# Layer 1's gelu as a tanh on ScalarE and a product on VectorE, with new ticks

## The chip, the cores and the metric

One of the eight cores of a Trainium2 chip runs the whole program. The metric is the device time of one execution in microseconds. The engines are called PE (TensorE, matrix products), ACT (ScalarE, functions of one operand), DVE (VectorE), POOL (GpSimd) and SP (the queue that issues the transfers).

## The reference, cut to what matters

Four layers are applied to x, 32 sequences (called items here) of 256 tokens by 256 channels: layer 0, two conditioned norms with a silu and a matrix product each; layer 1, a transformer block with 16 heads, an attention bias and a mask; layer 2, a stencil; layer 3, a causal transformer block. The change touches the feed-forward part of layer 1, whose width is 1024:

```
def _gelu2(x):
    return x * jax.nn.sigmoid(1.702 * x)
...
x = x + (ctx @ Wo + bo)
h = _ln(x) * g2 + beta2
ff = _gelu2(h @ W1 + b1) @ W2 + b2
return x + ff
```

Layer 3 has the same form with the exact gelu. It is identical in both kernels.

## The kernel before

All weights lie in SBUF, and the 32 items go through one long software pipeline. The order of the work is written out in ticks. Each piece of an item's work ("w1", "f1", ...) has a tick relative to the item's start; items start 64 ticks apart (PERIOD), and layer 3 of an item starts 160 ticks (S3) after its layer 1. The table P holds the ticks of the steady state, OWN replaces them for the first and last items, SPLIT has those that differ for attention in layer 3. Every engine goes through all the ticks in order and issues what falls on each; within one tick the attention comes first. So ticks set only the order of the instructions on each engine's queue. What waits for what across engines is set by semaphores. Attention has eight units per item and layer, four ticks apart, so one unit runs every four ticks.

The part around the change, for item b, with its ticks in P:

- Layer 1's rows of normed input are turned by PE into the bank bM (t2, 55). ACT writes their high half as fp16 into MB (t2_out, 52), and DVE the rest (t2_lo, 55). MB is the same tile as TN, which layer 3 of an earlier item uses in the same way (t4_out, lines 1370 to 1373, waits until layer 1's w1 has read MB).
- PE multiplies with W1 in four steps g, two ticks apart (w1, 57 to 63; line 1447), all into the one bank bM. After each step ACT copies it with its bias into AA[g], 128x512 fp32 as two halves (w1_out, 57 to 63; lines 1343 to 1347, the copy itself is line 1275). The next step on PE waits for that copy.
- ACT applies the gelu to each AA[g] in place (w1_gelu, 64; lines 1348 to 1352), four instructions of 128x512, with the per-tensor scale of the split weights. The function is Gelu_apprx_sigmoid, which needs a table of functions that the exp of the attention (line 1249) isn't in.
- PE multiplies AA[g] with W2 in four steps, one tick apart (w2, 68 to 71; line 1525 through `narrow`), each waiting for its gelu.
- DVE adds the result to x (f1, 74; line 1116), and the stencil of layer 2 follows from there (s_r, s_rp, ...; POOL has s_pm, s_b, s_ha).

Others that the prediction speaks of: DVE's `all_center` (line 969, pieces n1_center and n2_center), POOL's addition of the mask to the attention bias (mask_add, line 579, tick -23, 128x1024, one for each of the eight units), POOL's addition of a bias row to x (m1_b, line 617, tick 56), SP's load of the attention bias (ld_bt, -12), and WARM, which lists extra matmuls on a constant tile that PE executes at named places.

The four lines of the gelu:

```
for b in at(t, "w1_gelu"):
    for g in range(4):
        S.wait_ge(a_w1, 8 * b + 2 * g + 2)
        S.op.activation(AA[g][:, :], AA[g][:, :], ACT.Gelu_apprx_sigmoid,
                        scale=scale_of("w1", 0)).then_inc(a_h1, 1)
```

Of the kernel before, what the change touches and what calls it, by code (L numbers as in the profile page):

```python
# [49 lines left out]
def begin(layer, b):  # L50
# [6 lines left out]
    "score0": -1, "score1": -1, "bias0": 0, "bias1": 0, "exp0": 1, "exp1": 2, "flip0": 8, "flip1": 8, "ev0": 7,  # L57
    "ev1": 9, "pv": 14, "cx": 13, "ct": 17, "pvn": 17, "ld_bt": -12, "mask_add": -23, "stack": -8, "ld_x": -78,
    "ld_xn": -37, "ld_ab": -36, "ld_mask": -117, "mask": -34, "n1_stats": -75, "n1_ones": -69, "n1_sum": -69,
# [6 lines left out]
    "f1": 74, "s_pm": 63, "s_b": 67, "s_r": 75, "s_rp": 82, "s_re": 96, "s_ha": 81, "s_w": 97, "s_ab": 97,  # L66
    "s_row": 98, "s_mm": 103, "s_f": 103, "ld_w1": -24, "ld_sten": -46, "ld_w3": -277, "coefs": -21,
# [6 lines left out]
    "out": 74, "st_out": 71,  # L74
# [32 lines left out]
        "y3": 60, "m4_rstd": 249, "m4_b": 298, "ld_x": -76, "ld_xn": -71, "ld_ab": -70, "ld_mask": -17,  # L107
        "ld_bt_1": -13, "stack_1": -12, "s_row": 96, "stack_3": -39, "st_out": 840,
    },
# [7 lines left out]
        "t2_lo": 70, "f1": 89, "s_r": 94, "s_rp": 94, "s_re": 94, "s_ab": 99, "s_f": 104, "m3": -54, "t3_lo": -37,  # L117
# [7 lines left out]
        "m4_b": 656, "ld_x": -88, "ld_xn": -61, "ld_ab": -39, "ld_mask": -139, "ld_bt_1": -22, "stack_1": -17,  # L125
        "stack_3": 217, "st_out": 980,
    },
# [10 lines left out]
        "s_rp": 86, "s_re": 97, "s_w": 99, "s_ab": 102, "s_f": 109, "t3_lo": -44, "bias1_3": 0, "v3_out": 15,  # L138
# [1701 lines left out]
```

## Time and profile before

| what | us |
|---|---|
| median of 3 runs | 2604.91 (2603.47 to 2608.86) |
| the profiled execution | 2604.97 |
| its span, first to last instruction | 2603.7 |
| PE busy | 2470.5 |
| ACT busy | 2115.3 |
| DVE busy | 2043.6 |
| POOL busy | 1536.1 |

The durations below come from the profiled execution. The busy time of an engine is the time in which at least one of its instructions runs; matmuls are pipelined, and their ends are modelled. A timeline row has the start, the time up to the end of the last instruction of the row, and, in brackets, the idle time of the engine before it with what ended it.

### The profile page before, as it was taken

What the parts mean: (1) busy time and instruction counts of PE and PEld (TensorE: products, weight loads), DVE (VectorE), ACT (ScalarE), POOL (GpSimd) and SP (SyncE); (2) the same over time, 40 slices, a digit from 0 to 9 for tenths busy, and PEclk for the clock granted to TensorE, in tenths of its full rate; (3) what the DMA queues carried; (4) which work ended last, traced back from release to release, by engine and by line L of the source; (5) the groups of instructions that cost most, each with busy time, mean ns of one, the idle gap of its engine ahead of it and who ended that gap; (6) DMA issues with size and microseconds to landing.
All of it is one profiled execution on the core that took longest, in us unless ns stands there. A gap on an engine that the chain in (4) does not pass through costs nothing.

```text
span 2603.7 us, 57961 instructions
## 1 busy us (share of the span) xinstructions
PE 2470.5 (95%) x19148; PEld 2005.6 (77%) x19148; DVE 2043.6 (78%) x7387; ACT 2115.3 (81%) x4694; POOL 1536.1 (59%) x1487
## 2 busy tenths in 40 slices
PE   6878999999999999999999999999999999999987
PEld 5666778778877877887887788778878877877776
DVE  6787878788888778888787888878888888878653
ACT  2466888888898888889888888988888888888875
POOL 2566666556666656666665656666556576655421
PEclk6899999999999999999999999999999999999999
DMA  5433443333344333334443333444433344433211
GB/s 205 120 119 105 121 127 113 111 106 106 107 122 126 112 110 108 107 105 122 126 115 108 108 107 106 122 127 115 114 110 100 105 121 125 123 105 96 75 29 33
DMA packets 178537, 287.67 MB, mean 110 GB/s; under 512 B 46080, under 2 KB 99328, under 8 KB 177984
## 3 DMA queue, kind: packets, MB, share of 16 engines
q1 hardware_dynamic: 178240, 283.97, 38.5%
q8 instruction: 155, 2.54, 0.4%
q14 instruction: 142, 1.16, 0.2%
HBM read 174.64 MB, written 8.45 MB: 70 GB/s over the span
## 4 chain that ended last, share of the span: by engine, by line
PE 69%; DVE 15%; SPq 4%; ACT 4%; issue 3%; POOL 2%; DMA 2%; DVEq 0%; POOLq 0%; ACTq 0%
PE bank L1525 17%; PE bank L1447 12%; PE bank L1548 10%; PE bank L1538 6%; PE bank L1563 6%; PE bank L1507 6%; DVE PB L1010 4%; PE bank L1514 3%; SPq L496 3%; PE bank L1459 3%; PE bank L1701 2%; DVE bank L969 2%; PE bank L1436 2%; SPq L492 1%; DMA Ks<-KU 1%
## 5 line engine op out<-in xcount | busy, mean ns | idle before, releaser
L1249 ACT ACTIVATE PB<-PB,mx 128x256 f32<-128x256 f32 (+1 forms) x2048 | 831.4, 473 | 35.7 <-DVE mx L1010 34.7
L579 POOL TENSOR_TENSOR BT<-BT,MN 128x1024 f32<-128x1024 f32 x256 | 556.9, 2180 | 122.5 <-DMA BT<-in_bias 121.0
L1548 PE MATMUL bank<-ident,PB 128*128 128x128 f32 x3584 | 486.4, 274 | 11.5 <-ACT PT L1254 5.5
L1010 DVE CUSTOM_DVE_ANT_0 PB<-bank,BT 128x256 f32<-128x256 f32 x1024 | 372.0, 418 | 137.8 <-PE bank L1538 132.8
L1548 PEld LDWEIGHTS bank<-ident,PB 128*128 128x128 f32 x3584 | 421.6, 141 | 63.4 <-ACT PB L1249 10.6
L1447 PE MATMUL bank<-TN,WS_w 128*128 128x256 f16 x3072 | 378.8, 273 | 38.7 <-ACT BB L1275 19.6
L1538 PE MATMUL bank<-Ks,Qs 96*128 96x512 f32 (+1 forms) x1024 | 364.6, 430 | 25.5 <-DMA Ks<-KU 12.0
L1017 DVE COPY PT<-bank 128x512 f32<-128x512 f32 (+1 forms) x512 | 315.9, 617 | 87.5 <-PE bank L1548 85.8
L1447 PEld LDWEIGHTS bank<-TN,WS_w 128*128 128x128 f16 x3072 | 282.5, 98 | 120.1 <-ACT BB L1275 35.4
L1254 ACT ACTIVATE PT<-bank 128x512 f32<-128x512 f32 (+1 forms) x512 | 272.3, 532 | 94.9 <-PE bank L1548 90.6
L1010 DVE CUSTOM_DVE_ANT_0 PB<-bank,caus 128x128 f32<-128x128 f32 (+1 forms) x1024 | 306.6, 350 | 42.3 <-PE bank L1538 42.2
L1563 PE MATMUL bank<-PT,VW 128*32 128x256 f32 (+1 forms) x4096 | 248.2, 360 | 4.4 <-DVE CX L1027 2.4
L1525 PE MATMUL bank<-Wf,BB 128*128 128x256 f32 x1024 | 236.8, 379 | 0.8 <-ACT BB L1264 0.6
L1525 PE MATMUL bank<-Wf,AA 128*128 128x256 f32 x1024 | 236.0, 383 | 0.5 <-ACT AA L1351 0.4
L1538 PEld LDWEIGHTS bank<-Ks,Qs 96*128 96x128 f32 x1024 | 168.1, 192 | 67.7 <-DVE mx L1010 22.3
L1525 PEld LDWEIGHTS bank<-Wf,AA 128*128 128x128 f32 x1024 | 192.2, 191 | 29.5 <-issue 0.9
L1525 PEld LDWEIGHTS bank<-Wf,BB 128*128 128x128 f32 x1024 | 189.6, 190 | 25.1 <-issue 1.7
L1563 PEld LDWEIGHTS bank<-PT,VW 128*32 128x32 f32 x4096 | 107.5, 109 | 98.7 <-issue 49.0
L554 POOL TENSOR_SCALAR smm<-smm 128x2 f32<-128x2 f32 x32 | 7.2, 226 | 280.0 <-DVE smm L991 280.0
L1010 DVE DVE_READ_ACCUMULATOR2_ANT mx<- 128x1 f32 x2048 | 169.0, 83 | 0.0
L1275 ACT ACTIVATE BB<-bank,cols 128x256 f32<-128x256 f32 x256 | 107.4, 470 | 44.3 <-PE bank L1447 44.3
L1260 ACT ACTIVATE ET<-bank 128x256 f32<-128x256 f32 x256 | 97.2, 380 | 46.8 <-PE bank L1563 42.7
(285 smaller groups left out, 4735.9 us busy)
## 6 DMA issues: line engine op xcount, KB each, us to landing
BT<-in_bias SPq DMA_DIRECT2D x256, 512.0 KB, 4.3
Qs<-QH SPq DMA_DIRECT2D x512, 64.0 KB, 2.4
Ks<-KH SPq DMA_DIRECT2D x1024, 32.0 KB, 2.0
Qs<-QU SPq DMA_DIRECT2D x256, 64.0 KB, 2.4
Ks<-KU SPq DMA_DIRECT2D x512, 32.0 KB, 2.0
XT<-in_xT SPq DMA_DIRECT2D x32, 256.0 KB, 2.8
X<-in_x SPq DMA_DIRECT2D x32, 256.0 KB, 2.9
AB<-ada_rows SPq DMA_DIRECT2D x32, 256.0 KB, 3.7
```

The costliest lines, as they stand in the source:

```text
L579: G.op.tensor_tensor(v2(BT[k % 4]), v2(BT[k % 4]), MN[:, :].unsqueeze(1).broadcast_to([128, 2, 512]), ALU.add).then_inc(g_bt, 1)
L1010: V.op.tensor_tensor_reduce(PB[(2 * D + q) % 6][:, h * 256:h * 256 + w], bS[q][:, h * w:h * w + w], plus, -1.0, 3.0e38, ALU.add, ALU.min, ...
L1017: V.op.tensor_copy(flipped(u.D, 1)[:, 0:w], bP[1][:, 0:w]).then_inc(v_ev, 1)
L1249: S.op.activation(o, o, ACT.Exp, scale=-1.0, bias=mx[u.layer][:, c:c + 1]).then_inc(a_exp, 1)
L1254: S.op.activation(flipped(u.D, 0)[:, 0:w], bP[0][:, 0:w], ACT.Copy).then_inc(a_ev, 1)
L1275: S.op.activation(half(out, m), half(ps, m), ACT.Identity, scale=scale(m), bias=bias(m)).then_inc(sem, 1)
L1447: last = T.op.matmul(half(ps, m), w, v[:, k * 256:k * 256 + 256], start=(k == 0 and i == 0), stop=(k == 1 and i == 2))
L1507: last = T.op.matmul(half(ps, m), x[:, k * 256 + m * 128:k * 256 + m * 128 + 128], Wf[:, a + k * 256:a + k * 256 + 256], start=(k == 0), s ...
L1525: last = T.op.matmul(half(ps, q), x[:, f * 256 + q * 128:f * 256 + q * 128 + 128], Wf[:, c:c + 256], start=(g == 0 and f == 0 and q == 0), ...
L1538: T.op.matmul(bS[q][:, 0:2 * w].rearrange("p (h k) -> p h k", h=2), Qs[i][0:96, et * 256 + q * 128:et * 256 + q * 128 + 128], k2[:, :, 0:w ...
L1548: last = T.op.transpose(bP[h][:, c * 128:c * 128 + 128], PB[(2 * u.D + q) % 6][:, h * 256 + k * 128:h * 256 + k * 128 + 128], ident[:, :])
L1563: last = T.op.matmul(half(bV, J % 2)[32 * s:32 * s + 32, q:256], VW[x][:, v:v + 32], flipped(u.D - 1 + et, h)[:, k * 256:k * 256 + 256 - q ...
```

## The change

Layer 1's gelu is x * sigmoid(1.702 x) = 0.5 x (1 + tanh(0.851 x)). ACT now computes the tanh of a half (128x256) of AA[g] into a half of MB, eight times per item, and DVE computes (tanh + 1) * AA[g] in place (new piece h1, tick 67). The factor 0.5 goes into f1, which becomes a three-operand instruction with a pointer scalar. Two scales are made for this once, in the set-up. w2 waits for DVE's product (v_h1) and no more for ACT. MB is in use until the last product, so ACT's tanh waits for all four steps of w1, each tanh waits for the product of the half before last, and layer 3's t4_out waits for the products.

```
@@ def split_gains
+                if n == "w1":
+                    V.op.tensor_scalar(scale_of(n, 4), scale_of(n, 0), 0.851, None, ALU.mult).then_inc(v_ws, 1)
+                    V.op.tensor_scalar(scale_of(n, 5), scale_of(n, 0), 0.5, None, ALU.mult).then_inc(v_ws, 1)
@@ def middle (DVE)
+                for b in at(t, "h1"):
+                    for g in range(4):
+                        for i in range(2):
+                            V.wait_ge(a_h1, 8 * b + 2 * g + i + 1)
+                            V.op.scalar_tensor_tensor(out=half(AA[g], i), in0=half(MB, i), scalar=1.0, in1=half(AA[g], i),
+                                                      op0=ALU.add, op1=ALU.mult).then_inc(v_h1, 1)
                 for b in at(t, "f1"):
...
-                    V.op.tensor_tensor(x[:, :], bM[:, :], x[:, :], ALU.add).then_inc(v_f1, 1)
+                    V.op.scalar_tensor_tensor(out=x[:, :], in0=bM[:, :], scalar=scale_of("w1", 5), in1=x[:, :], op0=ALU.mult,
+                                              op1=ALU.add).then_inc(v_f1, 1)
@@ def scalar (ACT)
                 for b in at(t, "w1_gelu"):
+                    S.wait_ge(p_w1, 4 * b + 4)
                     for g in range(4):
                         S.wait_ge(a_w1, 8 * b + 2 * g + 2)
-                        S.op.activation(AA[g][:, :], AA[g][:, :], ACT.Gelu_apprx_sigmoid,
-                                        scale=scale_of("w1", 0)).then_inc(a_h1, 1)
+                        for i in range(2):
+                            S.wait_ge(v_h1, 8 * b + 2 * g + i - 1)
+                            S.op.activation(half(MB, i), half(AA[g], i), ACT.Tanh, scale=scale_of("w1", 4)).then_inc(a_h1, 1)
...
                 for b in at(t, "t4_out"):
-                    S.wait_ge(p_w1, 4 * min(b + 3, NB))
+                    S.wait_ge(v_h1, 8 * min(b + 3, NB))
@@ def tensor (PE)
                 for b, g in steps(t, "w2", 4, 1):
-                    T.wait_ge(a_h1, 4 * b + g + 1)
+                    T.wait_ge(v_h1, 8 * b + 2 * g + 2)
@@ WARM
-    "start": 24, "c1": 12, "n1_ones_0": 2, "v1": 9, "win_1": 5, "w1_0": 3, "n2_ones_2": 1, "n1_ones_3": 4,
-    "v1_3": 1, "v3": 10,
+    "start": 24, "c1": 12, "v1": 19, "v3": 9,
```

Nearly all the tables of ticks are replaced as well. In P, among others: w1 57 to 58 (w1_out stays at 57, w1_gelu at 64, w2 at 68), score1 -1 to 0, bias1 0 to 1, m1_b 56 to 39, mask_add -23 to -22, ld_bt -12 to -15, n1_center -62 to -66, n1_scale -61 to -60, f1 74 to 73, s_pm 63 to 64, y3 -8 to -45, xb -45 to -82. OWN, for the first and the last items, is replaced in most of its entries, and SPLIT is changed (among others its ct_3, at 16, goes, so that 17 holds for both layers).

## Rows read from the trace of the kernel before

**Rows 1.** The page: busy time and share by engine, and the granted clock in 40 slices.

```profile
PE 2470.5 (95%) x19148; PEld 2005.6 (77%) x19148; DVE 2043.6 (78%) x7387; ACT 2115.3 (81%) x4694; POOL 1536.1 (59%) x1487
...
PEclk6899999999999999999999999999999999999999
```

**Rows 2.** Busy time by stage: head, steady part, tail (window, length, each engine's busy us).

```profile
0.00:281.00 281.00, 220.99 (x1451) 174.36 (x1452) 212.48 (x690) 146.07 (x312) 142.08 (x139) 0.85 0.45 139
...
434.00:2331.00 1897.00, 1861.12 (x14706) 1518.78 (x14703) 1543.24 (x5626) 1639.98 (x3651) 1191.33 (x1151) 1.00 0.40 113
2331.00:2603.00 272.00, 239.00 (x1824) 191.52 (x1822) 163.93 (x624) 198.90 (x441) 106.49 (x107) 0.99 0.25 65
```

**Rows 3.** Waits of PE from 434 to 2331 us (total us, times, longest).

```profile
PE bank L1447 <- ACT BB L1275: 15.0, 25, 0.7
PE bank L1447 <- ACT AA L1275: 7.8, 24, 0.6
```

**Rows 4.** Groups of instructions on ACT: count, busy us, mean ns, idle before.

```profile
L1351 ACT ACTIVATE AA<-AA,ws 128x512 f32<-128x512 f32 x128 | 82.0, 711 | 0.4
L1249 ACT ACT_TABLE_LOAD x62 | 79.5, 1283 | 1.1
L1351 ACT ACT_TABLE_LOAD x32 | 41.1, 1283 | 0.6
```

**Rows 5.** Timeline of ACT (start us, duration us, instruction), around four layer-1 gelus.

```profile
434.81 2.56 ACT L1351 ACTIVATE AA<-AA,ws 128x512 f32<-128x512 f32 x4
...
1266.92 1.28 ACT L1351 ACT_TABLE_LOAD   x1
1268.21 2.56 ACT L1351 ACTIVATE AA<-AA,ws 128x512 f32<-128x512 f32 x4
1270.79 1.28 ACT L1249 ACT_TABLE_LOAD   x1
1272.09 0.91 ACT L1249 ACTIVATE PB<-PB,mx 128x256 f32<-128x256 f32 x2
...
1275.64 1.69 ACT L1249 ACTIVATE PB<-PB,mx 128x256 f32<-128x256 f32 x4
1277.24 0.58 ACT L1315 ACTIVATE bank<-FU 128x512 f32<-128x512 f32 x1
...
1343.75 2.56 ACT L1351 ACTIVATE AA<-AA,ws 128x512 f32<-128x512 f32 x4
...
2331.52 2.56 ACT L1351 ACTIVATE AA<-AA,ws 128x512 f32<-128x512 f32 x4
```

**Rows 6.** Timeline of PE at the start of w2.

```profile
1268.83 0.38 PE L1573 MATMUL bank<-ident,ET 128*128 128x128 f32 x2
1269.08 5.42 PE L1525 MATMUL bank<-Wf,AA 128*128 128x256 f32 x24
```

**Rows 7.** Timeline of POOL around the gelus of items 15 and 29.

```profile
1264.66 4.69 POOL L579 TENSOR_TENSOR BT<-BT,MN 128x1024 f32<-128x1024 f32 x2 [1.48 <-DMA BT<-in_bias]
1269.31 1.28 POOL L617 TENSOR_TENSOR X<-X,rows 128x512 f32<-128x512 f32 x1
...
2328.74 4.70 POOL L579 TENSOR_TENSOR BT<-BT,MN 128x1024 f32<-128x1024 f32 x2 [0.44 <-DMA BT<-in_bias]
```

**Rows 8.** Timeline of DVE around the gelu of item 15.

```profile
1266.17 1.18 DVE L969 SCALAR_TENSOR_TENSOR bank<-XT,sm,gT 128x512 f32<-128x512 f32 x1
...
1268.26 1.00 DVE L978 TENSOR_SCALAR FU<-bank,hs,hb 128x256 f32<-128x256 f32 x2
...
1274.78 0.42 DVE L1010 CUSTOM_DVE_ANT_0 PB<-bank,BT 128x256 f32<-128x256 f32 x1 [3.25 <-PE bank L1538]
```

**Rows 9.** Two DVE lines with two SBUF inputs: duration ns min/median/max.

```profile
L969 DVE SCALAR_TENSOR_TENSOR bank<-XT,sm,gT x64: 749/1759/2723, 19.0 to 2363.0; 128x512 f32<-128x512 f32 x64
...
L1155 DVE TENSOR_TENSOR AA<-AA x32: 682/684/686, 181.8 to 2511.9; 128x512 f32<-128x512 f32 x32
```

More of the change, by code:

```diff
@@ L56 @@
 P = {
-    "score0": -1, "score1": -1, "bias0": 0, "bias1": 0, "exp0": 1, "exp1": 2, "flip0": 8, "flip1": 8, "ev0": 7,
-    "ev1": 9, "pv": 14, "cx": 13, "ct": 17, "pvn": 17, "ld_bt": -12, "mask_add": -23, "stack": -8, "ld_x": -78,
-    "ld_xn": -37, "ld_ab": -36, "ld_mask": -117, "mask": -34, "n1_stats": -75, "n1_ones": -69, "n1_sum": -69,
[6 rows of a table removed]
-    "f1": 74, "s_pm": 63, "s_b": 67, "s_r": 75, "s_rp": 82, "s_re": 96, "s_ha": 81, "s_w": 97, "s_ab": 97,
-    "s_row": 98, "s_mm": 103, "s_f": 103, "ld_w1": -24, "ld_sten": -46, "ld_w3": -277, "coefs": -21,
[6 rows of a table removed]
-    "out": 74, "st_out": 71,
+    "score0": -1, "score1": 0, "bias0": 0, "bias1": 1, "exp0": 1, "exp1": 2, "flip0": 8, "flip1": 8, "ev0": 8,
+    "ev1": 9, "pv": 14, "cx": 14, "ct": 17, "pvn": 17, "ld_bt": -15, "mask_add": -22, "stack": -12, "ld_x": -96,
+    "ld_xn": -72, "ld_ab": -83, "ld_mask": -108, "mask": -53, "n1_stats": -81, "n1_ones": -68, "n1_sum": -69,
[6 rows of a table added]
+    "w1_gelu": 64, "h1": 67, "w2": 68, "f1": 73, "s_pm": 64, "s_b": 73, "s_r": 74, "s_rp": 81, "s_re": 87,
+    "s_ha": 73, "s_w": 98, "s_ab": 99, "s_row": 92, "s_mm": 103, "s_f": 103, "ld_w1": -24, "ld_sten": -46,
+    "ld_w3": -277, "coefs": -21, "split_p1": -55, "split_p1_hi": -50, "split_p1_lo": -45, "split_w1": -8,
+    "split_w1_hi": -4, "split_w1_lo": -2, "split_p3": 46, "split_p3_hi": 50, "split_p3_lo": 54, "split_w3": 82,
+    "split_w3_hi": 88, "split_w3_lo": 92, "film_a": -72, "film": -62, "adas": -57, "scr": -48, "m3": -45,
[4 rows of a table added]
 }
@@ L91 @@
     -2: {
[15 rows of a table removed]
-        "y3": 60, "m4_rstd": 249, "m4_b": 298, "ld_x": -76, "ld_xn": -71, "ld_ab": -70, "ld_mask": -17,
-        "ld_bt_1": -13, "stack_1": -12, "s_row": 96, "stack_3": -39, "st_out": 840,
[6 rows of a table added]
+        "t2_lo": 61, "h1": 75, "f1": 81, "s_r": 96, "s_rp": 96, "s_re": 97, "s_w": 99, "s_ab": 103, "s_f": 112,
[8 rows of a table added]
+        "ld_ab": -57, "ld_mask": -61, "ld_bt_1": -20, "stack_1": -18, "s_row": 88, "stack_3": -44, "st_out": 914,
     },
     -1: {
[6 rows of a table removed]
-        "t2_lo": 70, "f1": 89, "s_r": 94, "s_rp": 94, "s_re": 94, "s_ab": 99, "s_f": 104, "m3": -54, "t3_lo": -37,
[7 rows of a table removed]
-        "m4_b": 656, "ld_x": -88, "ld_xn": -61, "ld_ab": -39, "ld_mask": -139, "ld_bt_1": -22, "stack_1": -17,
-        "stack_3": 217, "st_out": 980,
-    },
[10 rows of a table removed]
-        "s_rp": 86, "s_re": 97, "s_w": 99, "s_ab": 102, "s_f": 109, "t3_lo": -44, "bias1_3": 0, "v3_out": 15,
[8 rows of a table removed]
-        "s_row": 93, "stack_3": -10, "st_out": 84,
-    },
[7 rows of a table removed]
-        "t2_lo": 62, "f1": 84, "s_r": 85, "s_rp": 92, "s_re": 92, "s_w": 98, "s_ab": 98, "s_f": 102, "m3": -38,
[7 rows of a table removed]
-        "ld_mask": -32, "ld_ab": -21, "ld_bt_1": 0, "stack_1": 4, "s_row": 100, "stack_3": -8, "st_out": 75,
[7 rows of a table added]
+        "s_rp": 92, "s_re": 93, "s_w": 95, "s_ab": 96, "s_f": 104, "m3": -56, "t3_lo": -40, "v3_out": 58,
[7 rows of a table added]
+        "m4_b": 662, "ld_mask": -142, "ld_x": -103, "ld_xn": -69, "ld_ab": -55, "ld_bt_1": -20, "stack_1": -14,
+        "s_row": 86, "stack_3": 103, "st_out": 1005,
+    },
[10 rows of a table added]
+        "h1": 72, "f1": 80, "s_r": 83, "s_rp": 87, "s_re": 95, "s_w": 99, "s_ab": 105, "s_f": 111, "m3": -47,
[6 rows of a table added]
+        "mask": -90, "mask_add_1": -71, "m1_rstd": -23, "m1_b": -4, "s_pm": 59, "s_b": 72, "s_ha": 75,
+        "m3_rstd": -65, "k3_lo": -37, "q3_lo": -26, "y3": -25, "m4_rstd": 35, "m4_b": 49, "scr": -309,
+        "ld_mask": -276, "ld_sten": -143, "ld_ab": -106, "ld_w1": -46, "ld_w3": -100, "ld_bt_1": -2, "stack_1": -2,
+        "s_row": 100, "stack_3": -7, "st_out": 80,
+    },
[7 rows of a table added]
+        "t2_lo": 59, "h1": 73, "f1": 77, "s_r": 84, "s_rp": 93, "s_re": 97, "s_w": 97, "s_ab": 98, "s_f": 102,
[7 rows of a table added]
+        "m4_b": 44, "ld_x": -234, "ld_xn": -265, "ld_mask": -31, "ld_ab": -44, "ld_bt_1": 0, "stack_1": 7,
+        "s_row": 102,
     },
@@ L168 @@
 SPLIT = {
-    "bias1_3": 1, "exp0_3": 2, "exp1_3": 3, "ev0_3": 8, "ev1_3": 10, "pv_3": 13, "cx_3": 12, "ct_3": 16,
-    "pvn_3": 18, "stack_3": -9,
+    "score1_3": -1, "bias0_3": 1, "exp1_3": 3, "ev1_3": 10, "pv_3": 13, "cx_3": 12, "stack_3": -18,
 }
@@ L291, in build @@
             "p_c1 a_c1 p_o1 v_m1 g_m1 p_t2 a_t2 p_w1 a_w1 a_h1 p_w2 v_f1")
-        g_s, v_s, d_row, p_s, v_m3, g_m3, p_t3, a_t3 = sems("g_s v_s d_row p_s v_m3 g_m3 p_t3 a_t3")
+        v_h1, g_s, v_s, d_row, p_s, v_m3, g_m3, p_t3, a_t3 = sems("v_h1 g_s v_s d_row p_s v_m3 g_m3 p_t3 a_t3")
         p_c3, a_c3, p_o3, v_t, g_t, p_t4, a_t4, p_w3, a_w3, a_ge, p_w4, v_o = sems(
@@ L362, in made @@
         def made(n):
-            steps = {"w1": 21, "p3": 31, "w3": 21}
+            steps = {"w1": 23, "p3": 31, "w3": 21}
             return sum(steps[m] for m in ORDER[:ORDER.index(n)])
@@ L374, in first_lo, with scaled @@
             return WP[:, 1536 + 512 * i:2048 + 512 * i]
+        def scaled(n):
+            return made(n) + len(split_of(n)[1]) + (13 if n == "w1" else 11)
         def scale_of(n, k):
@@ L913, in split_rest @@
                 first = sum(len(split_of(m)[1]) for m in ORDER[:ORDER.index(n)])
-                v0 = made(n) + len(parts) + 11
+                v0 = scaled(n)
                 ps = bM if n == "w1" else bT_
@@ L1294, in split_high @@
             def split_high(n):
-                k0 = made(n) + len(split_of(n)[1]) + 11
+                k0 = scaled(n)
                 S.wait_ge(v_ws, k0)
@@ L1486, in split_bias @@
                 ps = bM if n == "w1" else bT_
-                T.wait_ge(v_ws, made(n) + len(split_of(n)[1]) + 11)
+                T.wait_ge(v_ws, scaled(n))
                 if n == "p3":
```

136 rows, old and new, of tables (OWN, P) are left out of this document.

## The prediction

> **What bounds the kernel now.** I read the page's engine shares first: TensorE (PE) is busy 95% of the span, ScalarE (ACT) 81%, VectorE (DVE) 78%, and the granted clock reads 9 from the third of the 40 slices on, so the high level, 2.4 GHz [rows 1]. Then the stages: from 434 to 2331 us PE is busy 1861.1 of 1897 us, so 35.9 us of idle lie in 25 periods. The head (0 to 281) has 60.0 us of PE idle, the tail (2331 to 2603) has 33.0 [rows 2]. The period is the distance of the layer-1 gelus: 434.81 to 2331.52 is 25 items, 75.87 us each, and one of them by itself, 1268.21 to 1343.75, is 75.54 [rows 5]. So the steady part is a PE pipeline, and no other engine can give more there than what PE waits for it. PE's waits in that stretch say what that is: 15.0 + 7.8 us for ACT's copies out of the single PSUM bank between two steps of the wide layers [rows 3]. They are two thirds of the idle, 0.9 us per period. None of them names the gelu.
>
> **The change, part by part.** (1) *Table loads.* ACT loads a table of functions before each layer-1 gelu (32 times) and again before the exp behind it (31 of the 62 of that line); each lasts 1.283 us [rows 4]. Tanh needs none: the tanh of line 1315 starts at 1277.24, while the last exp before it ends (1275.64 + 1.69), so no load stands between them [rows 5]. So 64 loads less one or two, 81 us of ACT, go. In one period the block from the load to the next exp runs from 1266.92 to 1272.09, 5.17 us: a load, four gelus in 2.56, a load [rows 5]. In its place come eight 128x256 tanhs. The trace has no such instruction; the nearest rows are two exps of that size in 0.91 us back to back, 0.45 each [rows 5], and as the upper end 0.71, the 512-wide gelu [rows 4]. I take 0.45: 3.6 us. ACT waits for DVE's product of the half before last, so tanh, signal, product, signal repeat for two tanhs: 0.45 + 0.42 + about 0.2 is 1.1 us a pair, 4.3 for all. ACT gets 0.9 us per item, of an idle of some 10 us (257 us over 1897 [rows 2]).
>
> The rows put load and gelu directly behind each other (1266.92 + 1.28, gelu at 1268.21 [rows 5]), 1.3 us a switch. The Trainium skill's page ScalarE: Activation LUTs, section What ACT_TABLE_LOAD costs, has some 1380 ns of draining added to each load, 2.66 us in all; by that, an estimate from this page's figure, ACT would be freed of 64 x 2.66 = 170 us and gain some 3.6 us per item. The trace does not agree: the gelu starts 0.01 us behind the load, and the exp behind the gelus comes 1.32 us after them, one load.
>
> (2) *The product on DVE.* Eight 128x256 products with both inputs in SBUF. Two 128x256 scalings took 1.00 us, 0.50 each [rows 8]; a 512-wide operation on two SBUF tiles takes 0.684, so half of it, 0.34, is the lower end [rows 9]. I take 0.42: 3.4 us per item, DVE in the steady part from 1543 to 1543 + 25 x 3.4, 86% [rows 2]. The cover is DVE's own idle, of which 3.25 us stand in one piece behind this spot, from 1271.5 to 1274.78 [rows 8]. I cost it at nothing; without that cover the bias additions behind it would be up to 3.4 us late, and the next scores, which need their bank, with them.
>
> (3) *The moment at which w2 may start.* Its first matmul starts at 1269.08, 0.16 us behind the end of the first gelu (1268.21 + 0.71), and directly behind PE's transposes of 1268.83 [rows 4, 5, 6]. There is no slack here. Before, the first quarter is ready 1.28 + 0.71 = 2.0 us after ACT reaches the block; after, two tanhs, a product and two signals are 0.91 + 0.42 + 0.2 = 1.5 us. Uncontended that is 0.5 us earlier, of which PE can use nothing, since its own work is in front. The later quarters are ready every 1.1 us, and PE takes 24 matmuls, three quarters, in 5.42, 1.8 each [rows 6]. So only the first counts. But in the new order w1 starts at tick 58, not 57, and w2 still at 68: one tick of room, 1.2 us (75.87 / 64), is gone.
>
> (4) *f1* gets a pointer scalar. Between 0 and 0.07 us each (0.749, the quickest 512-wide three-operand form, against 0.684 [rows 9]). 32 of them, exposed for some seven items in head and tail: 0.5 us. The two new operations on one column in the set-up are once, beside transfers.
>
> (5) *Warm-up matmuls:* 14 go, 9 come, at most 0.2 us each (two 128-wide in 0.38 [rows 6]): 0 to -1 us, taken as -0.5. A lower clock stands in the first two slices alone [rows 1].
>
> (6) *Waits and queues.* The tanh's output lies in the tile that layer 1's wide layer reads, so ACT waits for all of w1 first; its w1_out of tick 63 needed that already. Layer 3's t4_out now waits for the product in place of w1, 21 ticks after it: free. ACT's third tanh waits for DVE to come to tick 67 while ACT is at 64; behind it stand the exps and the copies out of PSUM. POOL has m1_b moved from tick 56 to 39, ahead of three mask additions (ticks 42 to 50), and holds them until its norm of tick 51 is there, 13 ticks before the first is used; SP loads the bias three ticks sooner. Nothing waits for these in the steady rows [rows 3]. Bounds for all moved ticks: they can't give more than the PE idle of the steady part, and what a bad tick costs I bound by the same; I take 0.
>
> **The sum.** Steady part: ACT has a tenth more idle, so a tenth of the 22.8 us of waits for it: -2.3. Head and tail: seven items (0 to 3, 29 to 31) without full cover, each with 0 to 0.9 us earlier exps: -6.3 to 0, taken as -4, nearer to the full value as both loads stand on ACT's in-order queue. f1 +0.5, warm-ups -0.5. In all -6.3 us against the profiled execution's 2604.97 (span 2603.7), which is the median of the runs, 2604.91, to 0.1. That gives 2598.6, own range 2592 to 2606.
>
> **The rivals.** *A, the shared way into SBUF (slower).* While both engines read SBUF, they don't run side by side: the operation of line 969, with two SBUF inputs, takes 0.749 us at best, 1.759 in the median, 2.723 at most, while line 1155, a subtraction of two such tiles at another spot, has 0.682 to 0.686 [rows 9]. And POOL is there: two mask additions take 4.69 us from 1264.66, and m1_b follows [rows 7]; the same pair stands ahead of item 29's gelu (2328.74 + 4.70, gelu at 2331.52 [rows 5, 7]). DVE's 1.18 us at 1266.17 [rows 8] ends just past the first of them. The first product would stand at about 1267.5 and meet the second addition, which ends near 1269; then the first quarter is ready at about 1269.9, 0.8 us after w2's start of now. PE has nothing to do in between. It decides wherever the addition starts ahead of the product and lasts over 0.5 us more. 0.8 x 28 items = 22 us: 2627; where half of the items are hit, 2616. The Trainium skill's page SBUF — State Buffer, section Who interferes with whom, has the rule: a VectorE operation with two SBUF inputs and a GpSimd one that reads SBUF share a port, whoever is first keeps it for its whole length, and the other is blocked. The trace agrees in the rows of line 969. Against: POOL's order is new and DVE's tick 67 may fall between two additions. Chance 0.25.
>
> *B, the new order takes more of the waits away.* Of 35.9 us in the steady part and 93 in head and tail a seventh, 18 us: 2587. For it: one period is 75.54 and the mean 75.87, so 8 us over 25 are periods longer than that one [rows 5]. Against: no row shows which tick would do it. Chance 0.17.
>
> *C, ACT's relief is eaten by its new wait on DVE.* If DVE is 1 us behind ACT at tick 67, the block is 5.2 us again, and nothing changes: 2605. Chance 0.15.
>
> *D, tanh is put into another table than exp,* or the loads stay for another reason: 2608. The rows of line 1315 speak against it. Chance 0.03.
>
> **How the numbers follow.** The forecast has 0.40. A measurement of this kernel can tell some 0.2%, 5.2 us: faster is below 2599.7, slower above 2610. Faster: 0.24 of the forecast and all of B, 0.41. Same: 0.16 of the forecast, 0.02 of A, 0.10 of C, 0.01 of D, 0.29. Slower: 0.23 of A, 0.05 of C, 0.02 of D, 0.30. The range goes from 2582, which takes in B's size and a few us of the unknown ticks, to 2627, A's full price; about one in ten lies out on each side.
>
> **What would show it.** Right: 64 loads fewer; the tanh line near 0.45 us and with little idle before it; the product's mean duration under 0.6 us; w2's first matmul directly behind other PE work; PE idle of 33 us or less from 434 to 2331. Wrong, by A: products of 1 us and more in the mean, and waits of PE's line 1525 (w2) for DVE of some 0.8 us per item. Wrong, by B: period near 75.5, waits for ACT's line 1275 well under 20 us. Wrong, by C: ACT idle before tanh of 1 us per item, released by DVE.

## The result, and the profile after

The changed kernel takes 2874.64 us (median of 4 runs, 2872.61 to 2879.57), the kernel before 2605.12 beside it: a ratio of 1.1035, 95% interval 1.1019 to 1.1051. It is **10.3% slower**; 2598.6 was forecast, with a range from 2582 to 2627.

The page of the changed kernel: span, busy time and share by engine, the granted clock in 40 slices, and the chain that ended last by line.

```profile
span 2872.6 us, 58347 instructions
PE 2541.7 (88%) x19116; PEld 2017.9 (70%) x19116; DVE 2421.6 (84%) x7645; ACT 2071.0 (72%) x4758; POOL 1554.1 (54%) x1487
...
PEclk6889999999999999999999999999999999999999
...
DVE AA L1122 10%; PE bank L1462 7%; DVE PB L1016 7%; PE bank L1540 7%; PE bank L1563 5%; PE bank L1522 4%; PE bank L1578 4%; PE bank L1553 4%; DVE sme L1135 3%; DVE PT L1023 3%; ACT PB L1262 3%; PE bank L1716 2%; PE bank L1529 2%; PE bank L1451 2%; ACT AA L1288 2%
```

Read the engines against [rows 1]. ACT got its relief (2115.3 to 2071.0 us). DVE has 378 us more, where 3.4 us for each of 32 items, 109, were counted. PE is busy for 71.2 us more with nearly the same work (32 matmuls fewer on record), and idle for 330.9 us (2872.6 - 2541.7) where it was idle for 133.2, so 197.7 more. The new product heads the chain.

The groups of the changed kernel on DVE and ACT that answer for this (count, busy us, mean ns, idle before):

```profile
L1122 DVE SCALAR_TENSOR_TENSOR AA<-TN,AA 128x256 f32<-128x256 f32 x256 | 334.6, 1359 | 54.5 <-ACT TN L1367 54.4
L1135 DVE TENSOR_TENSOR sme<-X,er 128x8 f32<-128x8 f32 x64 | 56.8, 925 | 0.0
...
L975 DVE SCALAR_TENSOR_TENSOR bank<-XT,sm,gT 128x512 f32<-128x512 f32 x64 | 50.7, 792 | 0.0
...
L1367 ACT ACTIVATE TN<-AA,ws 128x256 f32<-128x256 f32 x256 | 125.1, 510 | 210.7 <-DVE AA L1122 210.4
L1277 ACT ACT_TABLE_LOAD x31 | 39.8, 1283 | 0.5
L1262 ACT ACT_TABLE_LOAD x30 | 38.5, 1283 | 0.5
```

A mean of 1359 ns for the product is not how long it works. Its line by itself has the spread (min/median/max in ns):

```profile
L1122 DVE SCALAR_TENSOR_TENSOR AA<-TN,AA x256: 409/1479/2350, 145.2 to 2760.3; 128x256 f32<-128x256 f32 x128
```

At its quickest it takes 409 ns, so 256 products are 105 us of work and 230 us of something else that the profile books as busy. What that is, the timelines of one item show, DVE first, then POOL, ACT and PE:

```profile
1313.23 11.06 DVE L1122 SCALAR_TENSOR_TENSOR AA<-TN,AA 128x256 f32<-128x256 f32 x7 [1.59 <-ACT TN L1367]
1324.52 0.43 DVE L1122 SCALAR_TENSOR_TENSOR AA<-TN,AA 128x256 f32<-128x256 f32 x1 [0.24 <-ACT TN L1367]
```

The first of these rows holds seven products. Windows cut closer show the second and the third of them:

```profile
1314.26 1.48 DVE L1122 SCALAR_TENSOR_TENSOR AA<-TN,AA 128x256 f32<-128x256 f32 x1
...
1315.66 2.35 DVE L1122 SCALAR_TENSOR_TENSOR AA<-TN,AA 128x256 f32<-128x256 f32 x1
```

```profile
1312.78 1.28 POOL L598 TENSOR_TENSOR X<-X,rows 128x512 f32<-128x512 f32 x1
1314.02 1.44 POOL L612 TENSOR_TENSOR X<-X,rows 128x512 f32<-128x512 f32 x1
1315.42 2.31 POOL L582 TENSOR_TENSOR BT<-BT,MN 128x1024 f32<-128x1024 f32 x1
1317.69 1.45 POOL L640 TENSOR_TENSOR Y<-X,rows 128x512 f32<-128x512 f32 x1
1319.27 4.40 POOL L582 TENSOR_TENSOR BT<-BT,MN 128x1024 f32<-128x1024 f32 x2
```

```profile
1314.43 0.51 ACT L1367 ACTIVATE TN<-AA,ws 128x256 f32<-128x256 f32 x1 [0.84 <-DVE AA L1122]
1315.78 0.51 ACT L1367 ACTIVATE TN<-AA,ws 128x256 f32<-128x256 f32 x1 [0.84 <-DVE AA L1122]
1318.11 0.51 ACT L1367 ACTIVATE TN<-AA,ws 128x256 f32<-128x256 f32 x1 [1.82 <-DVE AA L1122]
...
1323.98 0.51 ACT L1367 ACTIVATE TN<-AA,ws 128x256 f32<-128x256 f32 x1 [1.69 <-DVE AA L1122]
```

```profile
1315.89 1.96 PE L1540 MATMUL bank<-Wf,AA 128*128 128x256 f32 x8 [1.30 <-DVE AA L1122]
...
1319.47 1.99 PE L1540 MATMUL bank<-Wf,AA 128*128 128x256 f32 x8 [1.40 <-DVE AA L1122]
1324.00 3.65 PE L1540 MATMUL bank<-Wf,AA 128*128 128x256 f32 x8 [2.54 <-DVE AA L1122]
...
1327.72 1.89 PE L1540 MATMUL bank<-Wf,AA 128*128 128x256 f32 x8
```

Each tanh from the third on starts when a product has ended, so ACT's starts date the products. POOL's operations end at 1314.06, 1315.46 and 1317.73; the tanhs start at 1314.43, 1315.78 and 1318.11, some 0.3 to 0.4 us behind each. The two products shown by themselves end 0.28 us behind a POOL operation (1315.74 and 1318.01). One product gets through per POOL operation. With six POOL operations back to back, the seven products that start beside them take 11.06 us in place of 2.9, and PE waits in front of three quarters of w2.

It is so in the whole trace. Counted from the single instructions, 169 of the 256 products last over 0.5 us, and every one of them ends 0.28 us (0.275 to 0.287) behind the end of a POOL operation; the other 87 take 0.41 to 0.48 us.

The last fence shows the second loss: eight matmuls of w2 take 3.65 us at 1324.00 and 1.89 at 1327.72. The windows around them (length, then busy PE, PEld, DVE, ACT, POOL, and the granted clock):

```profile
1322.00:1324.00 2.00, 0.00 (x0) 0.00 (x0) 2.00 (x2) 0.31 (x2) 1.67 (x1) 1.00 0.14 29
1324.00:1326.00 2.00, 2.00 (x5) 1.63 (x6) 1.76 (x7) 2.00 (x6) 0.00 (x0) 0.50 0.00 0
```

PE stood idle for 2.54 us, and behind it the granted clock is 0.50, the level of 1.2 GHz. The mean granted clock is 0.970 against 0.984 before. So part of PE's waiting is paid a second time, as slower work.

PE's waits over the whole kernel (total us, times, longest):

```profile
PE bank L1540 <- DVE AA L1122: 126.8, 79, 2.6
PE bank L1553 <- DVE mx L1016: 72.1, 130, 4.7
PE bank L1462 <- ACT BB L1288: 18.1, 31, 0.9
```

The waits of [rows 3] are still there, but two others stand above them now: w2 for the product, which is new, and the scores for a bank that DVE empties (72.1 us; 10.6 before). Together they grew by 188 of the 197.7 us.

### The profile page after: what moved, and what is told of

The parts are those of the page before. It is cut to its first block, busy times and chain, and to the rows that moved or that the text cites. A ratio compares the mean times of both kernels' runs of the same rounds, so it can differ in the third digit from the quotient of the medians.

```text
span 2872.6 us, 58347 instructions
## 1 busy us (share of the span) xinstructions
PE 2541.7 (88%) x19116; PEld 2017.9 (70%) x19116; DVE 2421.6 (84%) x7645; ACT 2071.0 (72%) x4758; POOL 1554.1 (54%) x1487
## 3 DMA queue, kind: packets, MB, share of 16 engines
q8 instruction: 155, 2.54, 0.4%
## 4 chain that ended last, share of the span: by engine, by line
PE 38%; DVE 38%; ACT 11%; issue 6%; POOL 3%; SPq 2%; DMA 1%; DVEq 0%; ACTq 0%; POOLq 0%
DVE AA L1122 10%; PE bank L1462 7%; DVE PB L1016 7%; PE bank L1540 7%; PE bank L1563 5%; PE bank L1522 4%; PE bank L1578 4%; PE bank L1553 4%; DVE sme L1135 3%; DVE PT L1023 3%; ACT PB L1262 3%; PE bank L1716 2%; PE bank L1529 2%; PE bank L1451 2%; ACT AA L1288 2%
## 5 line engine op out<-in xcount | busy, mean ns | idle before, releaser
L1262 ACT ACTIVATE PB<-PB,mx 128x256 f32<-128x256 f32 (+1 forms) x2048 | 844.7, 472 | 28.8 <-DVE mx L1016 28.1
L1553 PE MATMUL bank<-Ks,Qs 96*128 96x512 f32 (+1 forms) x1024 | 393.8, 441 | 86.4 <-DVE mx L1016 72.1
L1462 PE MATMUL bank<-TN,WS_w 128*128 128x256 f16 x3072 | 382.4, 275 | 34.7 <-ACT BB L1288 18.1
L1540 PE MATMUL bank<-Wf,AA 128*128 128x256 f32 x1024 | 272.7, 415 | 126.8 <-DVE AA L1122 126.8
L1122 DVE SCALAR_TENSOR_TENSOR AA<-TN,AA 128x256 f32<-128x256 f32 x256 | 334.6, 1359 | 54.5 <-ACT TN L1367 54.4
L1540 PEld LDWEIGHTS bank<-Wf,AA 128*128 128x128 f32 x1024 | 204.0, 206 | 177.7 <-DVE AA L1122 102.9
L1367 ACT ACTIVATE TN<-AA,ws 128x256 f32<-128x256 f32 x256 | 125.1, 510 | 210.7 <-DVE AA L1122 210.4
L567 POOL TENSOR_TENSOR QU<-QU,QH 128x512 fp32r<-128x512 f32 x64 | 81.8, 1278 | 299.8 <-ACT QH L1305 299.8
```

Source lines behind the costliest of these rows:

```text
L1122: V.op.scalar_tensor_tensor(out=half(AA[g], i), in0=half(MB, i), scalar=1.0, in1=half(AA[g], i), op0=ALU.add, op1=ALU.mult).then_inc(v_h1, 1)
L1262: S.op.activation(o, o, ACT.Exp, scale=-1.0, bias=mx[u.layer][:, c:c + 1]).then_inc(a_exp, 1)
L1367: S.op.activation(half(MB, i), half(AA[g], i), ACT.Tanh, scale=scale_of("w1", 4)).then_inc(a_h1, 1)
L1462: last = T.op.matmul(half(ps, m), w, v[:, k * 256:k * 256 + 256], start=(k == 0 and i == 0), stop=(k == 1 and i == 2))
L1540: last = T.op.matmul(half(ps, q), x[:, f * 256 + q * 128:f * 256 + q * 128 + 128], Wf[:, c:c + 256], start=(g == 0 and f == 0 and q == 0), ...
L1553: T.op.matmul(bS[q][:, 0:2 * w].rearrange("p (h k) -> p h k", h=2), Qs[i][0:96, et * 256 + q * 128:et * 256 + q * 128 + 128], k2[:, :, 0:w ...
```

## The experiments

Theory T: a two-input operation of DVE in SBUF and an operation of POOL keep each other out, for as long as the one that is under way lasts. Against it stand theories in which POOL plays no part: the chain of tanh and product itself, DVE's extra 3.4 us of work, or the order of the new ticks. In the small-mask kernels line numbers are lower by 1.

**The two halves of the change.** First the new ticks with the old gelu:

```
 # before.py, with the new P, OWN, SPLIT and WARM
-    "n1_center": -62, "m1_b": 56, "s_re": 96, "y3": -8, "xb": -45, ...
+    "n1_center": -66, "m1_b": 39, "s_re": 87, "y3": -45, "xb": -82, ...
```

> The kernel before with the new tables of ticks alone (P, OWN, SPLIT, WARM); the gelu, its table loads and f1 as they were. Theory T (the products of h1 and POOL's reads of SBUF exclude each other): without products the new order is harmless, 2600 to 2620 us. Rival O (the new order itself is bad, whatever the gelu): most of the 270 us stays, 2780 us or more.

2683.74 us (2680.02 to 2684.9) against 2605.98 beside it, 1.0298 (1.0278 to 1.0318): **+78 us without any new operation**. That lies between the two forecasts and is a miss for both: theory T had said that without products the new order is harmless (2600 to 2620). It overlooked that the kernel has other operations of DVE with two inputs in SBUF. DVE and POOL in its trace, in one place:

```profile
1258.73 1.96 DVE L1122 TENSOR_TENSOR sme<-X,er 128x8 f32<-128x8 f32 x1
1260.61 0.15 DVE L1122 TENSOR_TENSOR sme<-X,er 128x8 f32<-128x8 f32 x1
```

```profile
1258.52 2.14 POOL L579 TENSOR_TENSOR BT<-BT,MN 128x1024 f32<-128x1024 f32 x1
```

An operation of 8 elements per row takes 1.96 us and ends just behind POOL's addition (1260.66); the next one, with nothing beside it, takes 0.15. They multiply the stencil's edges (s_re, moved from tick 96 to 87), in the mean 902 ns where they took 250 before. What such operations hold up is the scores, as PE's waits show:

```profile
PE bank L1538 <- DVE mx L1010: 55.2, 116, 4.7
...
PE bank L1525 <- ACT AA L1351: 12.2, 29, 1.0
```

The second row is step (3): with w1 at 58 and w2 still at 68 the first quarter of the gelu is late 29 times. Before, these waits came to 0.4 us, and those for the scores' bank to 10.6. The two grew by 56.4 us, about as much as PE is idle more (189.7 against 133.2); it is also busy for 23 us more.

The new ticks take one collision away, too. The operation of [rows 9] that had 1759 ns in the median, line 969, is line 975 in the changed kernel, and its mean is 792 ns there and was 1597 before, some 50 us less of DVE. They win no time that any run shows.

Then the new gelu with the old ticks:

```
 # after.py, with the old P, OWN, SPLIT and WARM, and
+    "h1": w1_gelu + 3
```

> The kernel after with the old tables of ticks, h1 three ticks behind w1_gelu. Theory T with POOL's order secondary: products still meet the mask additions; mean product 0.8 to 1.2 us, time 2680 to 2800. If POOL's bunch of additions at that place (new ticks) is the whole cause: mean product under 0.7 us, 2610 to 2650. Rival O: about 2605. Rival L (the ping-pong of ACT and DVE and 3.4 us more work on DVE are the cost, not the port): as slow as after, 2850.

2739.9 us (2736.0 to 2740.55), 1.0512 (1.0488 to 1.0535): **+134 us**. The time lies in T's range and outside those of the others. Products have a mean of 780 ns, just under T's 0.8 to 1.2 us:

```profile
L1122 DVE SCALAR_TENSOR_TENSOR AA<-TN,AA x256: 409/426/2390, 144.6 to 2628.8; 128x256 f32<-128x256 f32 x128
```

```profile
PE bank L1540 <- DVE AA L1122: 79.6, 40, 3.2
```

Three quarters of the products are undisturbed (median 426). 64 of the 256 last over 0.5 us, all of them until 0.28 us behind the end of a POOL operation, and the longest waits for nearly a whole mask addition. PE's waits for the scores' bank are 11.3 us here, as before the change: those came with the new ticks. 78 + 134 is 212 and the change costs 269.5: the halves make each other worse, by 58.

**POOL's long additions taken away.** The addition of the mask to the attention bias, 128x1024 and 2.1 us, is cut to eight columns; so nearly all of the mask is left out.

```
-G.op.tensor_tensor(v2(BT[k % 4]), v2(BT[k % 4]), MN[:, :]...broadcast_to([128, 2, 512]), ALU.add)
+G.op.tensor_tensor(BT[k % 4][:, 0:8], BT[k % 4][:, 0:8], MN[:, 0:8], ALU.add)
```

The changed kernel with it:

> The kernel after with POOL's mask addition cut from 128x1024 to 128x8, so the mask of nearly all of the bias is left out. Theory T: POOL has 550 us less to read, products come down to 0.7 us in the mean or less (the 1.28 us additions are left), time 2610 to 2700. Rival L: products and time stay, 2850 us.

The kernel before with it, as a control:

> The kernel before with the same cut of the mask addition, the control for the run above. PE bounds this kernel, so within 10 us of 2605 by both theories; line 969 on DVE comes down from a mean of 1.6 us towards 0.8 if T holds.

The new ticks alone:

> The new ticks with the old gelu, and POOL's mask addition cut from 1024 to 8 columns per unit (the mask is left out). The new ticks alone cost 78 us. Theory T (they cost that because they bring two-input operations of VectorE beside POOL's long ones, which shut each other out of SBUF): with the long operations gone most of it goes, 2608 to 2625 us against the 2602.9 of the control; the mean of the small bias row of the stencil (128x8, line 1122) falls from 902 to under 400 ns. Rival O (the new order is worse in itself, whatever POOL executes): 2650 us or more.

The new gelu alone:

> The new gelu with the old ticks, mask addition cut to 8 columns (the mask is left out). The new gelu alone costs 134 us. Theory T: most of it goes, 2608 to 2630 us, products 430 to 550 ns in the mean. Rival D (VectorE has 3.4 us more work per item and comes to the products too late, behind its norm pieces of ticks 66 and 67; POOL's additions matter little): 2660 us or more, with waits of PE's line 1540 for the products near the 79.6 us of the run with the mask.

One run each:

| us | mask addition whole | of 8 columns |
|---|---|---|
| before | 2605.12 | 2602.87 |
| new ticks | 2683.74 | 2627.44 |
| new gelu | 2739.9 | 2627.94 |
| both (the change) | 2874.64 | 2629.65 |

The control gains 2 us, the change 245. The mask additions cost the kernel before next to nothing, and 90% of the change's loss goes with them: +27 over the control are left of +269.5. PE's busy time comes back as well, from 2541.7 to 2468.0 us (2470.5 before the change). In the changed kernel the products' mean falls from 1359 to 586 ns, as T said (0.7 us or less). In the control the mean of line 969, here 968, falls from 1597 only to 1202, not quite towards 0.8, as POOL's additions of a bias row are left. Shortening the mask addition also hands DVE its bias sooner, but that isn't the gain: in the whole changed kernel DVE waited for it once, for 1.7 us. The extra cost of having both halves is gone too. For the ticks theory T had said 2608 to 2625; 2627.44 is a narrow miss (rival O, 2650 or more, is out). For the gelu 2627.94 lies in T's range, and rival D's 2660 is out. These are single runs, but the gaps to the rivals are over 20 us. The eight columns also take the small operation at s_re back to its size, and the products:

```profile
L1121 DVE TENSOR_TENSOR sme<-X,er 128x8 f32<-128x8 f32 x64 | 12.6, 238 | 0.0
```

is of the new ticks, 902 to 238 ns, and of the new gelu, 780 to 433 ns:

```profile
L1121 DVE SCALAR_TENSOR_TENSOR AA<-TN,AA 128x256 f32<-128x256 f32 x256 | 105.7, 433 | 26.7 <-ACT TN L1366 26.7
```

Only five products are held up there. DVE executes just as many instructions, so its amount of work was not the matter. Of the 25 us that each half still costs, PE's waits give most: for the gelu 20.9 us for the products, for the ticks 29.6 for the scores' bank (4.7 in the control) and 12.1 for the gelu at w2. What holds up the scores there wasn't tested; a second pair of edge operations, with the piece s_w, still lasts 592 ns in the mean beside another addition of POOL (192 before the change).

**One operand moved out of SBUF.** Whether it is SBUF that is disputed, two kernels tell that differ in one name. Both have the old ticks, four serial tanhs and products of 128x512, and w2 waits for all four:

```
-S.op.activation(MB[:, :], AA[g][:, :], ACT.Tanh, ...)    # twin: SBUF
+S.op.activation(bM[:, :], AA[g][:, :], ACT.Tanh, ...)    # PSUM bank of w2
-V.op.scalar_tensor_tensor(out=AA[g][:, :], in0=MB[:, :], scalar=1.0, in1=AA[g][:, :], ...)
+V.op.scalar_tensor_tensor(out=AA[g][:, :], in0=bM[:, :], scalar=1.0, in1=AA[g][:, :], ...)
```

> The kernel after with the old tables of ticks, four tanhs of 128x512 into the PSUM bank bM (free between w1's last copy and w2) and four products of 128x512, one after the other, w2 waiting for all four. The product has one input in SBUF. Theory T (shared way into SBUF): every product lasts 0.65 to 0.76 us, never over 0.8, whatever POOL does. Rival L: the same as in the twin run e6. By the serial chain, 4 x (0.6 + 0.7 + 0.15) = 5.8 us, w2 starts some 4 us later than before, so 2650 to 2740 us.

> The twin of e5: the same order, waits and sizes, but the tanh goes to the SBUF tile MB, so the product has two inputs in SBUF. Theory T: products between 0.68 and 2.8 us, mean 1.1 or more, and the run slower than e5 by 32 times the sum of four delays, 40 to 80 us. Rival L: as e5 within 0.5%.

The product's line in the first, and in the twin:

```profile
L1121 DVE SCALAR_TENSOR_TENSOR AA<-bank,AA x128: 678/692/693, 144.6 to 2737.4; 128x512 f32<-128x512 f32 x128
```

```profile
L1121 DVE SCALAR_TENSOR_TENSOR AA<-TN,AA x128: 685/807/2633, 143.7 to 2790.8; 128x512 f32<-128x512 f32 x128
```

With one input in PSUM all 128 products lie within 15 ns; with both in SBUF they reach 2633, at a mean of 1090 against 689. 128 x 0.401 us is 51 us; the times differ by 53 (2854.24, ratio 1.0944, 1.0914 to 1.0973; and 2907.69, 1.1151, 1.1124 to 1.1178). In the first, POOL's operations pass by without a trace; in the twin, the 64 products over 0.8 us all end 0.54 to 0.55 us behind one of them. This shows what theory T says of DVE, with one variable changed (the mean forecast for the twin, 1.1 us or more, was missed by 0.01). The forecast of the time for the first (2650 to 2740) missed by over 110 us:

```profile
PE bank L1538 <- DVE AA L1121: 176.5, 32, 6.9
```

5.5 us for each item, which is about the serial chain itself, four times 0.69 + 0.69; some 4 us of it had been counted. The rest of the 249 us is mostly PE at work: it is busy for 77 us more than before, at a mean granted clock of 0.948, which the forecast had left out. A chain of tanh and product in front of w2 that nothing hides costs its full length, with no collision in it. The bank used here is the one that w2 writes, so w2 has to wait for all four; another bank wasn't tried.

**Fewer, longer products.**

```
-for i in range(2): V.op.scalar_tensor_tensor(out=half(AA[g], i), in0=half(MB, i), ...)
+V.op.scalar_tensor_tensor(out=AA[g][:, :], in0=MB[:, :], ...)
```

> The new gelu with the old ticks, in four tanhs and four products of 128x512 through the whole tile MB, in place of eight of 128x256; w2 still starts behind the first quarter. In the run with eight, a product takes 780 ns in the mean against 410 alone, 3.0 us too much per item. Theory T (one wait for the port per instruction, of up to a whole POOL operation): about half as many waits, so 1.2 to 2.0 us too much per item over 4 x 685 ns, a mean of 0.98 to 1.2 us. Rival S (the two share the way in, and each byte is slower): the same 3.0 us too much, a mean of 1.43 us or more. The time: tanh and product no longer overlap (one tile), so 2730 to 2800 us, no faster than the 2739.9 of the run with eight.

```profile
L1121 DVE SCALAR_TENSOR_TENSOR AA<-TN,AA 128x512 f32<-128x512 f32 x128 | 133.3, 1042 | 83.9 <-ACT TN L1365 83.9
```

A mean of 1042 ns: 4 x (1.042 - 0.685) is 1.4 us too much per item where eight products had 8 x (0.780 - 0.41), 3.0. The mean is in T's range, and rival S, a price by the byte with a mean of 1.43 us or more, is out: 67 of the 128 products take 0.68 to 0.74 us, as long as alone or nearly. But that the waiting halves *because* the instructions do isn't shown. The other 61, all over 0.8 us, are about two for each item. In the run with eight small products 64 were over 0.5 us, also two for each item. As many were held up, each for a shorter time, and how long depends on how much of POOL's operation is left when the product comes. The time, 2752.03 (1.0556, 1.0529 to 1.0582), is as forecast no better, as tanh and product take turns on one tile.

**Which ticks.** The stencil's edges back behind POOL's additions, then POOL's early bias rows back in the changed kernel:

```
 # new ticks, old gelu
-    "s_re": 87,
+    "s_re": 96,
 # the changed kernel
-    "xb": -82, "y3": -45, "m1_b": 39, "q1_lo": -40,
+    "xb": -45, "y3": -8, "m1_b": 56, "q1_lo": -27,
```

> The kernel before with the new ticks (e1), but with the stencil's edge products on DVE (s_re) at 96 again, not 87. In e1 these 8-element operations with two SBUF inputs last 0.9 us in the mean against 0.21, since they now run beside POOL's s_ha. Theory T: they come back to 0.3 us or less and 20 to 60 of e1's 78 us go: 2625 to 2665. If e1's loss has other causes: 2684.

> The kernel after with four of POOL's pieces at their old ticks (xb -45, y3 -8, m1_b 56, q1_lo -27), all else new. In the trace of after, xb, x1_bo, y3 and four mask additions run back to back across the eight products. If this bunch makes the interaction (57 us above the sum of ticks alone and gelu alone): mean product from 1.36 to 0.8 to 1.0 us, time 2780 to 2830. If the order on POOL doesn't matter: 2875.

The one entry s_re gives back 23 of the 78 us: 2660.54 (1.0192, 1.0157 to 1.0227), in the range. The small operation's mean falls from 902 to 490 ns, not to the 0.3 us or less that was said: s_ha has moved too, and it meets that instead. PE's wait for the scores' bank falls from 55.2 to 30.6 us. In the second the products' mean came out as forecast, but the time was a miss: 2856.06 (1.0952, 1.092 to 1.0983), 18 us won of 269. Its two main waits:

```profile
PE bank L1553 <- DVE mx L1016: 123.0, 152, 4.7
...
PE bank L1540 <- DVE AA L1122: 35.7, 53, 2.7
```

The products fell to a mean of 962 ns, and w2's wait for them from 126.8 to 35.7 us as intended. But the scores' wait rose from 72.1 to 123.0. Taking one collision away moved the wait to the next, and why that one grew by so much wasn't tested.

**DVE told to come early.**

```
 # new gelu, old ticks
-    "h1": 67,
+    "h1": 65,
```

> The new gelu with the old ticks, and VectorE's products at tick 65 in place of 67 for the steady items, ahead of its norm pieces (n1_center 66, n1_scale 67). Rival D (the products are late because VectorE comes to them late): the wait of PE's line 1540 for the products falls from 79.6 to under 30 us, and the time from 2739.9 to 2690 or less. Theory T (POOL's two mask additions and its bias row stand there and hold the products, wherever VectorE's queue has them): the products' mean stays at 700 to 950 ns, and the time at 2715 to 2770 us.

2948.23 us (1.1303, 1.1278 to 1.1328), the slowest of all, and outside the times of both theories. Each was right in its other half: the products' mean is 936 ns, as T said, and w2's wait is short, as rival D said.

```profile
PE bank L1462 <- DVE HB L955: 259.4, 28, 10.6
...
PE bank L1540 <- DVE AA L1122: 8.4, 6, 2.6
```

w2's wait is nearly gone (79.6 to 8.4 us). In its place PE waits 28 times some 9.3 us for `HB`, the low half of layer 3's normed input, which stands on DVE's queue behind the products. The timelines of DVE and PE:

```profile
1340.61 3.69 DVE L1122 SCALAR_TENSOR_TENSOR AA<-TN,AA 128x256 f32<-128x256 f32 x3 [2.56 <-ACT TN L1367]
...
1348.27 0.43 DVE L1122 SCALAR_TENSOR_TENSOR AA<-TN,AA 128x256 f32<-128x256 f32 x1 [0.24 <-ACT TN L1367]
1348.62 0.68 DVE L955 TENSOR_TENSOR HB<-bank,HB 128x512 f16<-128x512 f32 x1
```

```profile
1349.36 2.74 PE L1462 MATMUL bank<-HB,WS_p 128*128 128x256 f16 x12 [9.63 <-DVE HB L955]
```

DVE idles 2.56 us for the first tanh, the eight products need 8.1 us, and only then comes the operation of 0.68 us that PE needs. Behind this idle time PE's 12 matmuls take 2.74 us at a granted clock of 0.50, and 1.48 elsewhere in the same trace. Two ticks of order on one queue are worth 208 us here. No version that computes the whole function beats the kernel before.

## Why the prediction was wrong, step by step

The forecast failed at two terms of its sum that were put at nothing: the product on DVE, step (2), and the moved ticks, step (6). By themselves they cost 134 and 78 us, and together 58 more.

- **Step (2), the product at nothing.** Alone it takes 0.41 to 0.43 us, as taken (0.42). But it was costed alone, beside a POOL that runs additions at that place. Booked at 1.36 us in the mean, eight products are 10.9 us of DVE, for which a cover of 3.25 us is no cover. The lateness also came elsewhere than the step said. It named the bias additions and the scores; with the new gelu alone these wait no longer than before (11.3 us against 10.6), and w2 waits for the product, 79.6 us. The 61.5 us more of the scores' wait came in with the ticks, 44.6 of them without any product.
- **Step (6), moved ticks at 0, bounded by PE's idle of the steady part.** This was the plainest fault: that bound holds for what ticks can give, and was used for what they can cost. The new ticks alone cost 78 us, 23 of them by one entry, s_re, which the step didn't look at. It looked at m1_b, which was moved back only together with xb, y3 and q1_lo (18 us for the four), so its own share isn't known.
- **Rival A named the mechanism, and its price was over 10 times too low.** It counted one collision per item, 0.8 us, from where one product would meet one addition. But all eight products are such instructions, POOL had six operations queued back to back, and a product went through behind each: 169 products were held up, over five for each item. In the item shown that is 11.06 us for seven, and over the kernel 230 us of DVE (334.6 busy, 105 of them work). The row that gave it away was in [rows 9]: the operation of line 969 was at 1.76 in the median, so collisions were its normal case, not a chance. What failed in the rival was one collision per item where several stood in a row, and the 0.25 that it was given.
- **Step (3), w2.** The tick of room lost showed up as 12.2 us of waits for ACT with the old gelu. With the product in the chain, the later quarters, said not to count, do: in the item shown PE waits 1.30 us for the first, 1.40 for the second and 2.54 for the third.
- **Step (1), table loads.** Right: 94 loads of lines 1249 and 1351 became 30, 64 fewer, and ACT is busy 44 us less (the tanh takes 0.51 us, where 0.45 was taken). The 6.3 us that the sum made of this relief are in no run. Its term of 2.3 us was a tenth of PE's waits for ACT's copies in the steady part; over the whole kernel these waits are 30.2 us before (19.6 + 10.6) and 30.2 after (18.1 + 12.1), and no shorter with the new gelu alone. ACT's queue now waits 210.4 us for the products. Rival C had 1 us per item for that; it is 6.6. Rivals B and D fell.
- **Step (5), warm-up matmuls.** The lists have 17 going and 10 coming, not 14 and 9. At the 0.2 us taken for one this is below what a run can tell.
- **The clock** wasn't in the sum. The sum priced idle time of PE only; 71 of the 270 us are PE at work, at a lower granted clock in places; w2's matmuls from AA alone went from 236.0 to 272.7 us. With the mask additions cut this goes with the waits (2468.0 us busy). How much of it is the clock wasn't measured by itself.

The signs named for A came true (products of 1 us and more; w2 waits for DVE), and the wait for w2 is 4.0 us per item in place of 0.8. The Trainium skill's page SBUF — State Buffer, section Who interferes with whom, has the rule that decides this case: a VectorE operation with two SBUF inputs and a GpSimd operation that reads SBUF exclude each other for a whole instruction. The runs agree for VectorE, by the PSUM twin (689 against 1090 ns) and by the 8-element operation of 1.96 us. Of GpSimd's side they show less: beside products of 0.41 us its operations last only 0.16 to 0.18 us longer.

## What to carry to other kernels

Before a two-input SBUF operation is given to VectorE, look at what GpSimd executes at that time: each such instruction, however small, may take its own time plus what is left of a GpSimd operation, up to a whole one. Where GpSimd has several queued up, this is paid again for each of them (169 of the 256 products were held up here). An operand in PSUM took the product out of the dispute. Half as many instructions of twice the size had half the waiting in them here, but won no time. And a table of ticks is a change of its own: its upside is bounded by the idle time of the bound engine, its downside is not.

## What the runs showed of the hardware that was not expected

- Against a queue of GpSimd operations, VectorE's products went through one at a time: 1.36 us in the mean for 0.41 of work. Each that was held up ended 0.28 us behind a GpSimd operation (0.54 to 0.55 us for products of 128x512). GpSimd pays as well, if less: the addition of a bias row, 128x512, takes 1.28 us in the median of the kernel before and took 1.44 between products; one of 128x1024 took 2.31 there, for 2.14 in the median before.
- An operation on 128x8 takes 0.15 us with nothing of GpSimd beside it and took 1.96 us beside a mask addition, so a small operation is not a cheap one.
- 2.54 us of idle PE were followed by a granted clock of 0.50, and eight matmuls in 3.65 us in place of 1.89.
